# First layer's expert results: weighted in the block and added by the scatter to a copy of x in DRAM

## The reference, cut to what matters

```python
def _L0_ffn_ref(x, Wr, br, ln_g, ln_b, W1, b1, W2, b2):
    logits = xt @ Wr + br
    top_p, top_idx = jax.lax.top_k(softmax(logits), 2)
    weights = top_p / top_p.sum(axis=-1, keepdims=True)
    xn = layernorm(xt)
    h = gelu(einsum('end,edh->enh', xn * ln_g + ln_b, W1) + b1)
    y = einsum('enh,ehd->end', h, W2) + b2
    return (weights * y[the two chosen experts]).sum(over the two)
...
x = x + _L0_ffn_ref(_layernorm(x), ...)
x = x + _L1_gnn_ref(_layernorm(x), ...)     # begins with the norm of the new x
```

## Time and profile before

| what | value |
|---|---|
| three runs, median (lowest, highest) | 2695.6 us (2692.14, 2705.16) |
| profiled execution | 2695.01 us |
| its span | 2693.3 us |
| TensorE matmuls, busy | 2127.6 us, 79% of the span |
| VectorE, ScalarE, GpSimd, busy | 1651.9, 1451.9, 1396.2 us |
| mean granted TensorE clock | 0.871 of full speed |
| route stage of the first layer | 877.6 to 930.9 us |
| experts' blocks | 931.8 to 1349 us |
| tail up to the start of the heads | 1349 to 1388.7 us |

### The profile page before, as it was taken

The page is one execution under the profiler, slowest core; times in us unless marked ns, Lnnn a source line. Parts: engine busy times, 40 slices in busy tenths (PEclk is TensorE's granted clock), DMA queues, the critical chain, the costliest instruction groups (busy, mean ns, idle before and its releaser), DMA issues. The chain is left out here.

```text
span 2693.3 us, 60550 instructions
## 1 busy us (share of the span) xinstructions
PE 2127.6 (79%) x15054; PEld 1744.7 (65%) x15055; DVE 1651.9 (61%) x4149; ACT 1451.9 (54%) x3568; POOL 1396.2 (52%) x1379
## 2 busy tenths in 40 slices
PE   4779966666767599999936889888885999679990
PEld 3666644444434499999924888787783777469990
DVE  8889963333333733333267877787877878843337
ACT  6779943333332443343346666666665888333335
POOL 0000067777777133333236777777752999236650
PEclk9989986767676699999967999999986999889995
DMA  3210036433333501111134787888863887552224
GB/s 114 96 58 21 22 89 198 137 106 106 105 105 101 202 32 35 35 37 37 41 110 149 242 240 238 247 242 240 241 199 107 268 269 240 191 183 70 70 66 147
DMA packets 181389, 365.89 MB, mean 136 GB/s; under 512 B 30058, under 2 KB 67348, under 8 KB 180990
## 3 DMA queue, kind: packets, MB, share of 16 engines
q1 hardware_dynamic: 118505, 208.65, 22.8%
q0 software_dynamic: 52608, 145.53, 19.6%
q10 hardware_dynamic: 10133, 9.97, 1.1%
HBM read 272.20 MB, written 91.83 MB: 135 GB/s over the span
## 5 line engine op out<-in xcount | busy, mean ns | idle before, releaser
L904 POOL DMA_INDIRECT weightsL_w<-y_gnn,all_slot_dst x416 | 396.0, 952 | 284.5 <-issue 282.7
L833 POOL DMA_INDIRECT scores_rows<-h_gnn,all_slot_dst x440 | 424.1, 964 | 141.7 <-issue 133.7
L963 PE MATMUL sum_ps<-weightsL_w 128*128 x880 | 341.9, 542 | 159.1 <-SPq L889 82.1
L963 PEld LDWEIGHTS sum_ps<-weightsL_w 128*128 128x128 f32 x880 | 217.4, 267 | 284.0 <-issue 250.4
L977 DVE TENSOR_TENSOR sums_acc<-sums_acc,sum_ps 128x256 f32 x440 | 185.5, 421 | 316.0 <-PE sum_ps L963 268.0
L1654 ACT ACTIVATE sums_acc<-expertsL_hid_ps,expertsL_b 128x128 f32<-128x128 f32 x704 | 197.6, 372 | 301.4 <-PE expertsL_hid_ps L1603 301.1
L1603 PE MATMUL expertsL_hid_ps<-sums_acc,expertsL_w 128*128 128x128 f32 x2816 | 337.4, 277 | 5.0 <-DVE sums_acc L1674 3.0
L2154 PE MATMUL scores_diff_ps<-all_ident,scores_rows 128*128 128x128 f32 x880 | 296.1, 337 | 48.1 <-DMA scores_rows<-h_gnn,all_slot_dst 40.3
L1603 PEld LDWEIGHTS expertsL_hid_ps<-sums_acc,expertsL_w 128*128 128x128 f32 x2816 | 327.2, 194 | 5.6 <-issue 5.5
L1615 PE MATMUL expertsL_out_ps<-weightsL_w,sums_acc 128*128 x1408 | 323.7, 380 | 0.0
L2156 PE MATMUL scores_diff_ps<-scores_minus,scores_node 128*128 128x128 bf16 x2640 | 309.6, 229 | 0.0
(11 more groups left out here) (456 smaller groups left out, 4235.1 us busy)
## 6 DMA issues: line engine op xcount, KB each, us to landing
saved_gnn<-scores_rows SPq DMA_DIRECT2D x220, 264.0 KB
sum_rows<-saved_gnn SPq DMA_DIRECT2D x220, 264.0 KB, 3.2
weightsL_w<-in_L_ffn_W SPq DMA_DIRECT2D x16, 1024.0 KB, 9.1
weightsL_w<-in_L_ffn_w SPq DMA_DIRECT2D x32, 512.0 KB, 9.8
scores_lanes<-slot_lanes SPq DMA_DIRECT2D x44, 320.0 KB
sort_low_b<-low_lanes SPq DMA_DIRECT2D x32, 416.0 KB, 4.5
weightsL_w<-ys_L SPq DMA_DIRECT2D x6, 1280.0 KB, 12.0
scores_rows<-h_gnn,all_slot_dst POOLq DMA_INDIRECT x440
```

What stands on the lines that cost most here:

```text
L833: pool.indirect_dma_start(out=self.rows[:, s, :], out_offset=None, in_=table[:, :], in_offset=bass.IndirectOffsetOnAxis(ap=e["slot_dst"][: ...
L904: pool.indirect_dma_start(out=rows[:, at:at + D], out_offset=None, in_=table[:, :], in_offset=bass.IndirectOffsetOnAxis(ap=e["slot_dst"][: ...
L963: last = nc.tensor.matmul(ps[(PAIRS * turn + s // 2) % len(ps)][:, s % 2 * D:(s % 2 + 1) * D], pick[h][:, s % HALF, :], rows[:, bass.ds(pl ...
```

## The change

In the first layer only, the weighting moves from the tail into the blocks, and the sum is made by the scatter in DRAM.

- Route stores x to a new DRAM tensor `sums` (row 128 + token; the 128 rows ahead of it take what empty lanes scatter), from SyncE's queue behind the expert weights; the semaphore is `begun`. ScalarE stores the 6400 weights to a DRAM list `weights` behind the route's other work, in two DMAs (`weights_kept`). The second moves 25 runs of 8 bytes per partition.
- At the start of the experts' stage VectorE computes the new scatter rows and the indices into the list (six short instructions). GpSimd waits for these, for `weights_kept` and for `begun` behind its first four gathers.
- For every block GpSimd gathers 128 weights (`bring_share`, 128 elements of 4 bytes), two blocks ahead. VectorE multiplies the bias by them, then makes (product times weight) plus that. The scatter adds (`compute_op=ADD`) to `sums`.
- The tail loads `sums` back into x in six parts and counts the statistics. ScalarE weighs nothing there.

```diff
+ in route, SyncE behind the weights:
+                if again:
+                    sp.wait_ge(joined, NT)
+                    sp.dma_start(rows(r["sums"], 0, 1), x[:, 0:1, :]).then_inc(r["begun"], 16)
+                    sp.dma_start(rows(r["sums"], 1, NT + 1), x[:, :, :]).then_inc(r["begun"], 16)
+ in route, ScalarE at its end:
+                if again:
+                    act.wait_ge(end, 1)
+                    nc.scalar.dma_start(r["weights"][0:1, :], c["ones"][0:1, 0:1]).then_inc(r["weights_kept"], 16)
+                    nc.scalar.dma_start(r["weights"][1:1 + TOP * NR, :].rearrange("(t p k) o -> p t (k o)", p=P, k=TOP), r["pairs"]).then_inc(r["weights_kept"], 16)
...
  in experts, GpSimd:
+                def bring_share(b):
+                    pool.indirect_dma_start(out=share[:, b:b + 1], out_offset=None, in_=r["weights"][:, :],
+                                            in_offset=bass.IndirectOffsetOnAxis(ap=slot[:, b:b + 1], axis=0)).then_inc(share_in[b % 2], 16)
                 for b in range(FEW):
                     bring(b)
+                if scaled:
+                    pool.wait_ge(indices, 2)
+                    pool.wait_ge(r["weights_kept"], 32)
+                    for b in range(2):
+                        bring_share(b)
+                    pool.wait_ge(r["begun"], 32)
...
+                        pool.indirect_dma_start(out=r["sums"][:, :], out_offset=bass.IndirectOffsetOnAxis(ap=r["result"][:, b:b + 1], axis=0),
+                                                in_=yb[:, b % 2, :], in_offset=None, compute_op=ALU.add).then_inc(y_out[b % 2], 16)
+                        if b + 2 < NB:
+                            bring_share(b + 2)
...
  in experts, VectorE's shift:
+                        if count is not None:
+                            ve.wait_ge(y_out[s], 16 * count)
+                        ve.wait_ge(share_in[s], 16 if count is None else 16 * count + 16)
+                        mine = share[:, bass.ds(b, 1)]
+                        nc.vector.tensor_scalar(yb[:, s, :], b2_sb[:, bass.ds(ex * D, D)], mine, None, ALU.mult)
+                        ve.drain()
+                        ve.wait_ge(product, 2 + b + 1)
+                        nc.vector.scalar_tensor_tensor(yb[:, s, :], out_ps[s][:, 0:D], mine, yb[:, s, :], ALU.mult, ALU.add).then_inc(done, 1)
...
+class Sums:
+    def load(self, sp, n):
+        tiles = self.PARTS[n]
+        sp.dma_start(self.target[:, tiles, :], rows(self.sums, 1 + tiles.start, 1 + tiles.stop)).then_inc(self.landed[n], 16)
+    def vector(self, ve, norm):
+        for n, tiles in enumerate(self.PARTS):
+            ve.wait_ge(self.landed[n], 16)
+            for t in range(tiles.start, tiles.stop):
+                self.nc.vector.bn_stats(norm.stats[:, t, :], self.target[:, t, :])
+        ve.drain()
```

More of the change, by code:

```diff
@@ L1224, in route @@
         pos_f = m.sb("pos_f", [P, TOP, NT])
[L1225 removed]
+        code = r["code"] if again else m.sb("code", [P, NB])
         masks = acc[:, 0:NT * D].bitcast(BF16)
@@ L1541, in experts @@
         y_out = [m.gather_sem(f"y_out{s}") for s in range(2)]
+        if scaled:
+            share = m.sb("share", [P, NB])
+            none = m.sb("none", [P, 1])
+            empty = m.sb("empty", [P, NB])
+            slot = m.sb("slot", [P, NB], I32)
+            share_in = [m.gather_sem(f"share_in{s}") for s in range(2)]
+            indices = m.sem("indices")
         turned, ready, hidden, acted, product, done, tick = (m.sem(n) for n in ("turned", "ready", "hidden", "acted", "product", "done", "tick"))
@@ L1771, in vector, with __init__ @@
         ve.drain()
+class Sums:
+    PARTS = Results.PARTS
+    def __init__(self, nc, m, r, target):
+        self.nc, self.sums, self.target = nc, r["sums"], target
+        self.landed = [m.sem(f"landed{n}") for n in range(len(self.PARTS))]
+    def load(self, sp, n):
[6 more added lines that the diff above has]
+                self.nc.vector.bn_stats(norm.stats[:, t, :], self.target[:, t, :])
+        ve.drain()
 class ToHeads:
@@ L1805, in scalar @@
         self.nc.scalar.activation(self.norm.root[:, 0:1], self.c["ones"][:, 0:1], ACT.Sqrt)
-        for n in range(len(self.results.PARTS)):
-            self.results.weigh(act, n)
+        act.drain()
         self.norm.root_of_var(self.nc, act)
@@ L2467, in feed_forward @@
     with Names(nc, f"ffn{tag}") as m:
-        r = dict(weight=m.sb("weight", [P, TOP, NT]), owner=m.sb("owner", [1, NB], I32),
-                 result=m.sb("result", [P, NB], I32), token=m.sb("token", [P, NB], I32))
-        ys_d = dram(f"ys_{tag}", [TOP * (N + 1), D])
         first = tag == "L0"
-        if not first:
-            r.update(z_scale=m.sb("z_scale", [P, NT]), z_shift=m.sb("z_shift", [P, NT]))
+        r = dict(owner=m.sb("owner", [1, NB], I32), result=m.sb("result", [P, NB], I32), token=m.sb("token", [P, NB], I32))
+        if first:
+            pairs = m.sb("pairs", [P, NT, TOP])[:, :, :]
+            r.update(pairs=pairs, weight=pairs.rearrange("p t k -> p k t"), code=m.sb("code", [P, NB]),
+                     sums=dram("sums_L0", [P + NR, D]), weights=dram("weights_L0", [1 + TOP * NR, 1]),
+                     begun=m.sem("begun"), weights_kept=m.sem("weights_kept"))
+            ys_d = None
+        else:
+            r.update(weight=m.sb("weight", [P, TOP, NT]), z_scale=m.sb("z_scale", [P, NT]), z_shift=m.sb("z_shift", [P, NT]))
+            ys_d = dram(f"ys_{tag}", [TOP * (N + 1), D])
         z_d = dram(f"z_{tag}", [NR, D])
```

26 lines of the change are left out of this document (21 added, 5 removed).

## The result

The changed kernel takes 2687.16 us, the median of 20 runs (2683.04 to 2694.84); the kernel before, timed beside it, 2691.95 us (20 runs). The ratio of the two is 0.9973, interval [0.9961, 0.9984]: faster beyond the noise, by 0.27% (the two medians alone give 0.18%), but within the half per cent that I had called "no change". Predicted was 2683 us in a range of 2675 to 2692, so the forecast of the time holds. Its sum does not: I had 12.7 us less, the medians give 4.8 and the two spans 6.9 (2693.3 and 2686.4 us). Two of its terms were wrong, in opposite directions, and the base was high: over 20 runs the kernel before takes 3.6 us less than the 2695.6 that I started from.

What follows compares the result with a forecast made beforehand. The prediction took TensorE to bound the first layer's blocks and VectorE's work behind the load the tail; -19.0 + 2.4 + 0.1 + 3.8 = -12.7 us from 2695.01 gave 2682.3, as a median 2683 us, range 2675 to 2692.

Steps and rivals of the forecast that it cites:

- The tail, what is removed: Tail: 18.0 us of VectorE work and half the bytes go, the load is late next; ends 19.0 us earlier.
- The last two scatters: Stage's end, ahead of the tail's load: adding scatters cost 1.2 us more each, +2.4 us (ends 0 and +7.6).
- the other figure in the prediction, 0.2 us each: Last two scatters: the skill's average HBM access, 0.2 us; by it alone the two would cost +0.4 us.
- Rival C: Adding scatters dear but hidden, turnaround 6 to 7.2 us: +5 to +7.6 us at the end, 2687 us; 18%.
- The copy of x, a wait that gets longer: Route: x's copy shares DMA engines with z's stores, so the masks start later, +3.8 us (ends 0 and +4.3).
- Rival B: Route: z not held up, x's copy runs in z's gaps and behind it, masks on time, 2679 us; 14%.
- The weight list, "Cost 0": Route's end: list takes 2.4 to 9 us; the gathers waiting for it may start 23 us after issue; cost 0.
- The blocks: First layer's blocks: GpSimd's third indirect DMA and VectorE's extra 0.36 us fit into TensorE's 7.24 us period; cost 0.
- The sum: Whole kernel: -19.0 + 2.4 + 0.1 + 3.8 = -12.7 us against 2695.01 us, so 2682.3.

Runs made afterwards that it cites:

- the doubled kernel: Changed kernel with a second adding scatter of every block, to a spare DRAM tensor, ahead of the real one and waited for: 3139.49 us beside 3053.04, ratio 1.0295.

## Why the prediction was right or wrong

- *The tail, what is removed.* Right in mechanism, -18.1 for -19.0. The step that was off is the end: I let the last packet decide, with five statistics behind it. In fact VectorE had 20 statistics to run when the third part landed, 7 us behind the load's issue. The rate of 0.35 us for one, from the earlier trace rows, was right (6.74 / 20 = 0.34).
- *The last two scatters.* Right in place, +2.1 for +2.5, and the value came out by luck, as two errors cancel. Against the kernel before, each link costs 0.6 us more and not 1.2, and 0.9 us more passes ahead of the first, which I had not counted. The base was misread too: scatter 55 did not wait for a landing alone, since VectorE's result came 0.76 us ahead of its start as it did for scatter 54. The add itself costs 1.4 us in the last link, more than the 1.2 that I took, and far more than the other figure in the prediction, 0.2 us each. Rival C (dear adds) is out: the links are 4.1 to 4.2 us, not 6.
- *The copy of x, a wait that gets longer.* Wrong: +3.8 for 0. The step that failed is its first sentence, "issued behind the last weights (891.46)". SyncE's program has a wait for `kept` between the weights and the new lines. That wait cost nothing before, since nothing stood behind it, but it was there to be read, in the code and in SyncE's own waits between 885 and 935 us of the kernel before:

```profile
SPq L1245 <- DMA z_L<-sums_acc: 23.8, 1, 23.8
```

Rival B named the right outcome, masks on time, for a wrong reason, the gaps of z. Moved ahead of the wait, the copy costs 5.5 us, against the 3.8 that I had: the sharing itself was argued rightly and sized too low.
- *The weight list, "Cost 0".* Wrong: 5.3 us at the first turn by the list alone in the kernel before, 7.2 us of the stages by taking its pieces away from the changed one. I had followed who waits for the list (GpSimd, whose slack of 23 us was real: it waited 5.6 us and TensorE never for that) and not who shares the engines with it. The first gathers and loads of the next stage run just then, and the earlier trace rows had them. I had also bounded the list's end by the share of engine time of a packet, 12 to 45 ns, and so by 9 us. By that measure its pieces are cheap, 7.6 ns each, and still the list landed 12.4 us after its issue (931.3 to 943.7), which is 62 ns of elapsed time for each of an engine's 200 pieces. The share of time does not bound the landing.
- *The blocks.* Right: TensorE at 395.00 of 395.00 us. GpSimd's share is 210.28 × 7.24 / 395 = 3.9 us of a period.
- *The sum.* From -12.7: the tail +0.9, the scatters -0.4, the copy -3.8, the start of the blocks +7.2, the start of the heads +0.4, small ones -0.4, so -8.8 for the -8.9 of the stage. So that 2683 came out near 2687 is in part luck: a cost that did not arise and a cost not foreseen partly cancel (-3.8 and +7.2). The base of 2695.6 us, 3.6 too high, helped as well. Of the 12.7 us forecast, the medians show 4.8.

## What to carry to other kernels

When a DMA is added at a stage's end, list what else is in flight in the ten us behind it, on all queues, and not only who waits for its own semaphore; and count its pieces as well as its bytes: here 25 KB in 3200 pieces held up the next stage by 5 to 7 us, and in 128 runs not at all. Read the issuing engine's program down to the new line, and price each wait that stands ahead of it, those that cost nothing before above all; the queue's own waits show them. An accumulating scatter in place of a reload shortened the tail by 18 us and cost only 2 at its end, since the loop is bound by TensorE and has by estimate some 3 us per block in which to hide it.

## What the runs showed of the hardware

- A store of 3200 pieces of 8 bytes (25 KB) landed 12.4 us after its issue, and 432 unrelated packets took 262 ns each of engine time meanwhile (12 ns without it); as 128 runs of 200 bytes the same bytes left the first turn where it was, at 5.0 to 5.3 us. The Trainium skill (DMA: Bandwidth & Descriptors, Specifications) says that transfers below 512 bytes become read-modify-writes. This would fit, but the runs of 200 bytes lie below that too and went well; no run here separates size from count.
- An adding scatter of 128 rows of 1 KB: 144 packets and some 1.3 us of movement against 48 and 0.4; landing 4.4 us against 2.7; start to the dependent start 4.1 to 4.2 us at the stage's end (4.1 to 4.6 in the doubled kernel) against 2.8 for the plain one in its place. Its instruction took 1.6 to 2.2 us (median 1.86) against 0.99 to 1.87 (median 1.40) for the plain one in its place.
- The granted clock fell to 0.50 in a pause of 3 us between two groups of products, though the products ahead of it had ended at a clock of 1.00, and the products behind it took 5.15 to 6.72 us for the same 32 instructions in different kernels.
